# A graph attention kernel: each group's row of destinations spread by a DMA from HBM instead of by broadcast matmuls into PSUM

## The chip, the cores and the metric

One core of a Trainium2 chip runs the whole program in one launch. The metric is the device time of that launch in microseconds; the kernel before takes 2448.84 us, the median of 3 runs (2448.01 to 2454.68). The changed kernel is timed in the same way on the same inputs.

## What is computed

A two-layer graph transformer over 3125 nodes (D = 128, 8 heads of 16) and 100000 edges, sorted by destination, plus one self loop per node; a last residual and layer norm follow. Cut to what matters:

```python
for l in range(L):                       # L = 2
    xn = _layernorm(x, ln1_g[l], ln1_b[l])
    deg = segment_sum(1, src); deg = (deg - deg.mean()) / (std(deg) + 1e-06)
    xp = xn + xn @ Wpos[l] + bpos[l] + deg[:, None] * Wdeg[l][0] + bdeg[l]
    q, k, v = (xp @ Wq[l] + bq[l]), (xp @ Wk[l] + bk[l]), (xp @ Wv[l] + bv[l])
    att = clip(einsum('ehd,ehd->eh', q[dst], k[src]) / 4, -50, 50)
    alpha = softmax of att over the edges of one dst
    aggr = segment_sum(v[src] * alpha, dst)
    x = x + (aggr @ Wo[l] + bo[l])
    h = gelu(_layernorm(x, ln2_g[l], ln2_b[l]) @ W1[l] + b1[l])
    x = x + (h @ W2[l] + b2[l])
return _layernorm(x_first + x)
```

## The kernel before, in words

The nodes stand in NT = 25 tiles of 128 rows, `x` and `qkv` in SBUF throughout. The edges are cut into NG = 98 groups of GE = 1024 (8 chunks of 128). Each engine has its own instruction stream, written out by hand, and the streams meet through counting semaphores only.

Before the layers, the two edge rows are loaded (SP, L352 and L353), node degrees are counted by one-hot matmuls (L956), and for each group the first and last destination tile are found; a (group, tile) pair is numbered, and `pair_words` reads from a table how many pairs each group has (244 pairs in the 196 groups of both layers, 1.24 tiles a group). A layer then runs:

1. Dense start: normalise, transpose and project each tile to q, k, v (L1010, L1016). SP stores k and v to a table in HBM, five tiles at a time (L382, ten stores over both layers). ScalarE and VectorE split q into three bf16 parts (`q_parts`).
2. The edge stage, over the 98 groups:
   - GpSimd (L452) issues, for each group, eight indirect DMAs that gather 128 rows of 1 KB (k and v of the sources) into one of SLOTS = 4 buffers of `kv`. It waits for `idx_ready` and, for a buffer's reuse, for `msg_done` of the group four earlier.
   - TensorE `broadcast_rows` (L1035): the group's 1024 destination numbers stand in one partition of `dst_hi` and `dst_lo` (multiples of 128 and the rest, both exact in bf16). A `pick` matrix that is one in that row spreads them over 128 partitions, four matmuls of 512 columns into two PSUM banks. It is issued two groups ahead, after `picked` and after `dist_done` says that the banks are free. Groups 0 to 97 have it; the last two steps of the loop issue none.
   - ScalarE `one_hots` (L563, L566): for each pair, |destination - node| (`dist`), then relu(1 - that), which gives the one-hot `hotT`; before it `pick_rows` (L535) prepares `pick` for two groups ahead.
   - TensorE `gather_q` (L1048): 24 bf16 matmuls a pair give q[dst] in PSUM.
   - VectorE: product with gathered k (L830), sum over a head (L835), clip (L842 to L845); the second one-hot `hot` (L812); after ScalarE's exp (`weights`, L570) the product with v (L854), which raises `msg_done`.
   - TensorE `sum_pair` (L1062): 8 fp32 matmuls a pair (16 records) add the group's messages to its destination tile; VectorE adds the result to `acc` (L808).
3. Dense end: quotient, output projection (L1101, L1106), second layer norm, the two matrices of the feed-forward part (L1114, L1120), with GpSimd adding biases (L466).

ScalarE's order in the edge stage is: exp of group g, one-hots of group g + 2, exp of group g + 1, and so on. SP has nothing to do in the edge stage, but for the second copy of x (L386, L387), which overwrites the q part of `qkv` in layer 1 once that isn't read any more and is waited for (`first_in`) by VectorE before the feed-forward part of layer 1.

Of the kernel before, what the change touches and what calls it, by code (L numbers as in the profile page):

```python
# [21 lines left out]
BF16 = mybir.dt.bfloat16  # L22
# [16 lines left out]
SLOTS = 4  # L39
UN = 5  # L40
# [22 lines left out]
def gnn_program(nc, x_d, src_d, dst_d, W, out_d):  # L63
    ctx = ExitStack()
    with ctx:
# [24 lines left out]
        dst_hi = sb("dst_hi", [NG, GE], BF16)  # L90
        dst_lo = sb("dst_lo", [NG, GE], BF16)
# [13 lines left out]
        pick = sb("pick", [NG, 2, P], BF16)  # L105
# [51 lines left out]
        tmp_i = row_buf(5, I32)  # L157
        tmp_j = row_buf(6, I32)
# [34 lines left out]
        dst_rows = ps[:, 6:8, :].rearrange("p b n -> p (b n)")  # L193
# [22 lines left out]
        dst_split = sem("dst_split")  # L216
        dst_parts = sem("dst_parts")
# [41 lines left out]
        row_ready = sems("row_ready")  # L259
# [16 lines left out]
        picked = sems("picked")  # L276
# [72 lines left out]
        def _(sp):  # L349
# [22 lines left out]
            for l in range(L):  # L372
# [3 lines left out]
                load(b2_bc[:, l, :], W["b2"][l, :].partition_broadcast(P), kept_in)  # L376
            for l in range(L):

                table = kv_tab[l][:, :].rearrange("(t p) d -> p t d", p=P)
                with sp.Fori(0, NU) as i:  # L380
                    sp.wait_ge(qkv_done[l], UN * i + UN)
                    sp.dma_start(table[:, bass.ds(UN * i, UN), :], qkv[:, bass.ds(UN * i, UN), D:3 * D]).then_inc(tab_out[l], 16)  # L382
            sp.wait_ge(self_msg, L * NU)
# [19 lines left out]
        def _(pool):  # L403
            pool.memset(src_i, -1).then_inc(rows_clear, 1)
            pool.memset(dst_i, -1).then_inc(rows_clear, 1)
            pool.memset(x[:, NT - 1, :], 0.0).then_inc(x_clear, 1)
# [63 lines left out]
        def _(act):  # L470
# [21 lines left out]
            act.wait_ge(dst_split, 1)  # L492
            nc.scalar.activation(dst_hi[:, :], tmp_i, ACT.Copy, scale=float(P)).then_inc(dst_parts, 1)
            nc.scalar.activation(dst_lo[:, :], tmp_j, ACT.Copy).then_inc(dst_parts, 1)
# [24 lines left out]
            for l in range(L):  # L519
# [13 lines left out]
                def pick_rows(g):  # L533

                    nc.scalar.activation(pick[:, bass.ds(g % 2, 1), :], spread(ident[0:NG, at(g)], 2, P), ACT.Copy).then_inc(picked[l], 1)  # L535

                pick_rows(0)
                pick_rows(1)

# [14 lines left out]
                def one_hots(word, d, g):  # L554
# [3 lines left out]
                    act.wait_ge(row_ready[l], g + 1)  # L558
                    pick_rows(g + 2)
                    with act.Fori(a, b) as pr:  # L560
                        t = tile_of(act, pr, shift)
                        act.wait_ge(hotT_ready[l], pr + 1)
                        nc.scalar.activation(dist[:, :], dst_rows, ACT.Abs, bias=neg_node[:, at(t)]).then_inc(dist_done[l], 1)  # L563
# [10 lines left out]
                one_hots(word, 0, 0)  # L574
# [574 lines left out]
```

## Time and profile before

| | us |
|---|---|
| median of 3 runs (all: 2454.68, 2448.84, 2448.01) | 2448.84 |
| span of the profiled execution | 2449.8 |
| TensorE matmul busy | 1621.6 (66%) |
| TensorE weight load busy | 1408.2 (57%) |
| VectorE busy | 1418.8 (58%) |
| ScalarE busy | 807.7 (33%) |
| GpSimd busy | 1603.8 (65%) |
| data moved by DMA | 219.86 MB, 90 GB/s |

The page gives the span of one profiled execution, which is 1.0 us above the median of the runs; the page gives no time for what lies around the span. A busy share is an average over stages: the dense stages and the edge stage have different limits. So the page is read from its part 4, the chain that ended last, and then by asking what each engine's idle time ended with. PE is TensorE, PEld its weight loads, DVE is VectorE, ACT ScalarE, POOL GpSimd, SP SyncE; a trailing q marks an engine's sequencer. A busy GpSimd does not move the gathered data; it prepares the descriptors, and the DMA engines move the rows.

### The profile page before, as it was taken

Reading aid. Unit: us, or ns where it says so; the run is one execution under the profiler, and the core shown is the slowest. Engines: PE = TensorE matmul, PEld = TensorE weight load, DVE = VectorE, ACT = ScalarE, POOL = GpSimd, SP = SyncE. Lnnn points to the kernel's source line nnn. Section 1 sums busy time; section 2 is a strip of 40 time slices with the busy share of each in tenths; the row PEclk is TensorE's granted clock in tenths of the full one; section 3 lists DMA queues with packets and bytes.
Section 4 is the critical chain, followed back from the end, with each engine's and each line's share of the span. In section 5 each row is a group of like instructions: output and inputs, shape, how many; then the busy total and the mean of one; then the engine's idle time right before and its main releaser. Section 6 shows DMA issues by size and latency. Waiting matters only on the chain.

```text
span 2449.8 us, 47166 instructions
## 1 busy us (share of the span) xinstructions
PE 1621.6 (66%) x12557; PEld 1408.2 (57%) x12558; DVE 1418.8 (58%) x2438; ACT 807.7 (33%) x1355; POOL 1603.8 (65%) x1686
## 2 busy tenths in 40 slices
PE   0995656666666666666687555666666666676767
PEld 0983555555555555666675455555555656665667
DVE  3448555555556666666655655555555555565664
ACT  0004323233333333333356322333333333333326
POOL 2005777777777777777713777777777777777721
PEclk9997878887788888888888787778888888888878
DMA  1103333333333333333301433333333333333310
GB/s 48 24 1 95 105 101 103 102 102 101 105 101 101 102 103 102 102 104 101 103 1 65 125 101 101 103 101 103 103 101 101 102 103 102 102 105 101 103 37 27
DMA packets 92154, 219.86 MB, mean 90 GB/s; under 512 B 27615, under 2 KB 40068, under 8 KB 92106
## 3 DMA queue, kind: packets, MB, share of 16 engines
q0 software_dynamic: 75072, 205.10, 29.0%
q1 hardware_dynamic: 17034, 14.14, 1.9%
q8 instruction: 28, 0.46, 0.1%
q14 instruction: 20, 0.16, 0.0%
HBM read 210.98 MB, written 8.15 MB: 89 GB/s over the span
## 4 chain that ended last, share of the span: by engine, by line
POOL 61%; issue 21%; PE 11%; DVE 2%; DMA 2%; SPq 1%; POOLq 1%; DVEq 0%; ACT 0%; ACTq 0%
POOL kv L452 61%; PE ps L956 4%; PE ps L1114 2%; PE ps L1120 2%; PE ps L1016 1%; DMA x<-in_x 1%; SPq L353 1%; PE ps L1062 1%; DMA kv<-kv_tab,idx 0%; PE ps L1010 0%; DVE stats L626 0%; PE ps L1106 0%; DVE qkv L750 0%; DMA kv_tab<-qkv 0%; DVE x L897 0%
## 5 line engine op out<-in xcount | busy, mean ns | idle before, releaser
L452 POOL DMA_INDIRECT kv<-kv_tab,idx x1564 | 1539.0, 984 | 494.2 <-issue 475.2
L1062 PE MATMUL ps<-msg,hot 128*128 128x136 f32 x3904 | 754.7, 370 | 669.1 <-DVE msg L854 557.5
L1062 PEld LDWEIGHTS ps<-msg,hot 128*128 128x128 f32 x3904 | 700.9, 268 | 768.4 <-issue 768.0
L830 DVE TENSOR_TENSOR prod<-kv,ps 128x1024 f32<-128x1024 f32 x196 | 239.4, 1221 | 705.3 <-DMA kv<-kv_tab,idx 696.6
L1048 PE MATMUL ps<-q_parts,hotT 128*128 x5856 | 423.4, 235 | 58.8 <-issue 42.0
L1048 PEld LDWEIGHTS ps<-q_parts,hotT 128*128 x5856 | 402.8, 108 | 81.4 <-issue 68.1
L570 ACT ACTIVATE msg<-att 128x64 f32<-128x64 f32 x196 | 50.2, 256 | 1112.8 <-DVE att L845 1108.8
L812 DVE TENSOR_TENSOR hot<-node_row,dst_col 128x1024 f32 (+1 forms) x244 | 299.2, 1226 | 97.0 <-issue 97.0
L563 ACT ACTIVATE dist<-ps,neg_node 128x1024 bf16<-128x1024 f32 x244 | 271.9, 1114 | 51.9 <-issue 37.2
L566 ACT ACTIVATE hotT<-dist 128x1024 bf16 x244 | 257.8, 1057 | 44.1 <-ACT dist L563 44.1
L835 DVE TENSOR_REDUCE dots<-prod 128x64 f32<-128x1024 f32 x196 | 239.1, 1220 | 0.3
L854 DVE TENSOR_TENSOR msg<-kv,msg 128x1024 f32<-128x1024 f32 x196 | 238.9, 1219 | 0.1
L1035 PE MATMUL ps<-dst_hi,pick 98*128 98x512 bf16 x392 | 150.5, 384 | 6.0 <-issue 5.0
L1035 PE MATMUL ps<-dst_lo,pick 98*128 98x512 bf16 x392 | 149.8, 382 | 0.0
L466 POOL TENSOR_TENSOR x<-x,b_bc 128x128 f32 x50 | 22.7, 456 | 139.5 <-ACT z L487 139.5
L535 ACT ACTIVATE pick<-ident 98x128 bf16 (+1 forms) x200 | 61.4, 308 | 158.2 <-issue 96.6
L956 PE MATMUL ps<-q_parts 128*64 128x49 bf16 x784 | 98.2, 302 | 4.7 <-DVE q_parts L704 4.7
L956 PEld LDWEIGHTS ps<-q_parts 128*64 128x64 bf16 x784 | 97.2, 221 | 7.0 <-DVE q_parts L704 4.8
L443 POOL TENSOR_TENSOR x<-x,bo_bc 128x128 f32 x50 | 24.9, 500 | 92.3 <-ACT z L487 91.9
L808 DVE TENSOR_TENSOR acc<-acc,ps x244 | 70.3, 288 | 14.9 <-PE ps L1062 8.3
L703 DVE TENSOR_TENSOR q_parts<-q_parts,qkv 128x1792 bf16<-128x1792 bf16 x28 | 30.6, 1092 | 64.5 <-PE ps L956 63.9
L601 ACT ACTIVATE kv<-ps,b1f 128x128 f32<-128x128 f32 x200 | 57.2, 369 | 20.5 <-PE ps L1114 20.5
(156 smaller groups left out, 1058.8 us busy)
## 6 DMA issues: line engine op xcount, KB each, us to landing
kv<-kv_tab,idx POOLq DMA_INDIRECT x1564
kv_tab<-qkv SPq DMA_DIRECT2D x10, 640.0 KB, 3.3
out<-x SPq DMA_DIRECT2D x4, 320.0 KB
hot<-in_L_gnn_W SPq DMA_DIRECT2D x2, 256.0 KB
w<-in_L_gnn_W SPq DMA_DIRECT2D x2, 256.0 KB, 3.3
kv<-in_src SPq DMA_DIRECT2D x1, 388.0 KB
kv<-in_dst SPq DMA_DIRECT2D x1, 388.0 KB
out<-x SPq DMA_DIRECT2D x1, 256.0 KB
```

Of the source, the lines that this page charges most:

```text
L452: pool.indirect_dma_start(kv[:, u, c, :], None, kv_tab[l][:, :], bass.IndirectOffsetOnAxis(ap=idx[:, u, c:c + 1], axis=0)).then_inc(kv_in[ ...
L563: nc.scalar.activation(dist[:, :], dst_rows, ACT.Abs, bias=neg_node[:, at(t)]).then_inc(dist_done[l], 1)
L566: nc.scalar.activation(hotT[:, bass.ds(pr % 2, 1), :], dist[:, :], ACT.Relu, bias=1.0, scale=-1.0).then_inc(hotT_ready[l], 1)
L808: nc.vector.tensor_tensor(acc[:, at(t), :], acc[:, at(t), :], agg[:, bass.ds((end + 1) % 2, 1), :], ALU.add).then_inc(evac_done[l], 1)
L812: nc.vector.tensor_tensor(hot[:, u % 2, :, :], spread(node_row[:, bass.ds(t * P, P)], 1, GC), dst_col[:, :, at(g)].broadcast_to([P, GC, P] ...
L830: nc.vector.tensor_tensor(prod[:, :].rearrange("p (c d) -> p c d", d=D), kv[:, u, :, 0:D], qd[u % 2].rearrange("p (c d) -> p c d", d=D), A ...
L835: nc.vector.tensor_reduce(dots[:, :], prod[:, :].rearrange("p (n d) -> p n d", d=HD), AX.X, ALU.add).then_inc(dot_done[l], 1)
L854: nc.vector.tensor_tensor(half[:, :, 0:D].rearrange("p c (h d) -> p c h d", d=HD), kv[:, u, :, D:2 * D].rearrange("p c (h d) -> p c h d", ...
L956: last = MM(cnt, hot_lo[b][:, :, c], hot_hi[b][:, :, c], start=False, stop=True, skip_group_check=True)
L1035: last = MM(dst_rows[:, cut], pick[:, gp, :], part[:, cut], start=start, stop=not start)
L1048: last = MM(qd[u % 2][:, c * P:(c + 1) * P], hotT[:, bass.ds(pr % 2, 1), c * P:(c + 1) * P], q_parts[:, at(t), k * D:(k + 1) * D], start=f ...
L1062: last = MM(agg[:, bass.ds(pr % 2, 1), :], hot[:, u % 2, c, :], msg[:, u % 2, c, :], start=(c == 0), stop=(c == GC - 1))
```

## The change

The destination row no longer goes through TensorE. The 1024 int32 numbers of group g are read from HBM by one DMA on SP whose source has a step of zero over 128 partitions, so each partition receives the same 4 KB (512 KB a group, 196 loads over both layers). They land in one of ROWS = 3 buffers of a new SBUF tile `dst_rows`, [128, 3, 1024] int32. ScalarE's `dist` reads that buffer, as int32 from SBUF instead of fp32 from PSUM. `pick`, `dst_hi`, `dst_lo`, the two VectorE instructions that split the numbers (L656, L657), the two of ScalarE that convert them (L493, L494) and all `broadcast_rows` are gone. GpSimd clears `dst_rows` at the start. SP issues the load of group g after the exp of group g - 4 (the first three of a layer at once, behind that layer's table stores), and its later work, the next layer's stores and the second copy of x, stands behind the loads. ScalarE's loop is unrolled by six groups instead of four.

```diff
+ROWS = 3
+TURN = 2 * ROWS
-        dst_hi = sb("dst_hi", [NG, GE], BF16)
-        dst_lo = sb("dst_lo", [NG, GE], BF16)
+        dst_rows = sb("dst_rows", [P, ROWS, GE], I32)
-        pick = sb("pick", [NG, 2, P], BF16)
-        dst_rows = ps[:, 6:8, :].rearrange("p b n -> p (b n)")
+        rows_in = [sems(f"rows_in{l}_", ROWS) for l in range(L)]
...
+            sp.wait_ge(rows_clear, 3)
             for l in range(L):
 
                 table = kv_tab[l][:, :].rearrange("(t p) d -> p t d", p=P)
                 with sp.Fori(0, NU) as i:
                     sp.wait_ge(qkv_done[l], UN * i + UN)
                     sp.dma_start(table[:, bass.ds(UN * i, UN), :], qkv[:, bass.ds(UN * i, UN), D:3 * D]).then_inc(tab_out[l], 16)
+                for g in range(NG):
+                    r = g % ROWS
+                    if g >= ROWS:
+                        sp.wait_ge(exp_done[l], max(1, g - ROWS))
+                    elif l:
+                        sp.wait_ge(exp_done[l - 1], NG)
+                    n = min(GE, E - g * GE)
+                    sp.dma_start(dst_rows[:, r, 0:n], dst_d[g * GE:g * GE + n].partition_broadcast(P)).then_inc(rows_in[l][r], 16)
...
+            pool.memset(dst_rows[:, :, :], -1).then_inc(rows_clear, 1)
...
-            act.wait_ge(dst_split, 1)
-            nc.scalar.activation(dst_hi[:, :], tmp_i, ACT.Copy, scale=float(P)).then_inc(dst_parts, 1)
-            nc.scalar.activation(dst_lo[:, :], tmp_j, ACT.Copy).then_inc(dst_parts, 1)
...
-                def pick_rows(g):
-
-                    nc.scalar.activation(pick[:, bass.ds(g % 2, 1), :], spread(ident[0:NG, at(g)], 2, P), ACT.Copy).then_inc(picked[l], 1)
-
-                pick_rows(0)
-                pick_rows(1)
...
-                def one_hots(word, d, g):
+                def one_hots(word, d, r, n):
 
                     a = word(d - 1)[0]
                     b, shift = word(d)
-                    act.wait_ge(row_ready[l], g + 1)
-                    pick_rows(g + 2)
+                    act.wait_ge(rows_in[l][r], 16 * (n + 1))
                     with act.Fori(a, b) as pr:
                         t = tile_of(act, pr, shift)
                         act.wait_ge(hotT_ready[l], pr + 1)
-                        nc.scalar.activation(dist[:, :], dst_rows, ACT.Abs, bias=neg_node[:, at(t)]).then_inc(dist_done[l], 1)
+                        nc.scalar.activation(dist[:, :], dst_rows[:, r, :], ACT.Abs, bias=neg_node[:, at(t)]).then_inc(dist_done[l], 1)
...
-            nc.vector.tensor_single_scalar(tmp_i, dst_i, 7, ALU.arith_shift_right)
-            nc.vector.tensor_single_scalar(tmp_j, dst_i, P - 1, ALU.bitwise_and).then_inc(dst_split, 1)
...
-                def broadcast_rows(gp, g, a):
-
-                    pe.wait_ge(picked[l], g + 1)
-                    if a is not None:
-                        pe.wait_ge(dist_done[l], a)
-                    for half in range(2):
-                        cut = slice(512 * half, 512 * half + 512)
-                        for part, start in ((dst_hi, True), (dst_lo, False)):
-                            last = MM(dst_rows[:, cut], pick[:, gp, :], part[:, cut], start=start, stop=not start)
-                    last.then_inc(row_ready[l], 1)
```

## Rows read from the trace of the kernel before

**Rows 1.** The page, part 4: shares of the chain that ended last, by engine.

```profile
POOL 61%; issue 21%; PE 11%; DVE 2%; DMA 2%; SPq 1%; POOLq 1%; DVEq 0%; ACT 0%; ACTq 0%
```

**Rows 2.** Groups by line: L452: busy us, mean ns | idle before, releasers.

```profile
L452 POOL DMA_INDIRECT kv<-kv_tab,idx x1564 | 1539.0, 984 | 494.2 <-issue 475.2 <-DMA kv_tab<-qkv 18.3 <-DVE idx L728 0.6
```

**Rows 3.** Line L452: count, duration min/median/max in ns.

```profile
L452 POOL DMA_INDIRECT kv<-kv_tab,idx x1564: 942/946/2000, 217.2 to 2347.0; - x196
```

**Rows 4.** The chain in order of time, layer 0: start us, us, what.

```profile
360.05 1.97 POOL kv L452
...
401.43 1.96 POOL kv L452
```

**Rows 5.** The page, part 5: groups of L563, L1035 and L535.

```profile
L563 ACT ACTIVATE dist<-ps,neg_node 128x1024 bf16<-128x1024 f32 x244 | 271.9, 1114 | 51.9 <-issue 37.2
...
L1035 PE MATMUL ps<-dst_hi,pick 98*128 98x512 bf16 x392 | 150.5, 384 | 6.0 <-issue 5.0
...
L535 ACT ACTIVATE pick<-ident 98x128 bf16 (+1 forms) x200 | 61.4, 308 | 158.2 <-issue 96.6
```

**Rows 6.** Groups by line, small ones: L493, an int32 row read from SBUF.

```profile
L493 ACT ACTIVATE dst_hi<-kv 98x1024 bf16<-98x1024 int32 x1 | 1.1, 1057 | 38.7 <-DVE kv L657 38.7
```

**Rows 7.** Timeline, start of the kernel: start us, us, engine, line, what, idle.

```profile
0.81 0.95 POOL L404 MEMSET kv<- 98x1024 int32 x1 [0.29 <-POOLq L1135]
...
38.76 4.01 POOL L430 TENSOR_SCALAR kv<-kv 98x1024 f32<-98x1024 f32 x1 [27.87 <-DVE kv L655]
...
42.99 4.93 DVE L626 BATCH_NORM_STATS2 stats<-x 128x6 f32<-128x128 f32 x25 [2.28 <-DMA x<-in_x]
```

**Rows 8.** The page, DMA issues by line: KB each, median us to landing.

```profile
kv_tab<-qkv SPq DMA_DIRECT2D x10, 640.0 KB, 3.3
...
bo_bc<-in_L_gnn_bo SPq DMA_DIRECT2D x2, 64.0 KB, 3.6
```

**Rows 9.** Layer 0's start: ScalarE's first `dist`, VectorE's first product, 33rd gather.

```profile
226.45 1.11 ACT L563 ACTIVATE dist<-ps,neg_node 128x1024 bf16<-128x1024 f32 x1 [0.19 <-issue]
...
235.91 1.22 DVE L830 TENSOR_TENSOR prod<-kv,ps 128x1024 f32<-128x1024 f32 x1 [1.19 <-issue]
...
258.75 0.95 POOL L452 DMA_INDIRECT kv<-kv_tab,idx  x1 [0.30 <-issue]
```

**Rows 10.** Layer 1's end: exp of group 93, VectorE's first zT copy.

```profile
2314.97 0.26 ACT L570 ACTIVATE msg<-att 128x64 f32<-128x64 f32 x1 [3.99 <-DVE att L845]
...
2385.78 0.61 DVE L909 COPY zT<-ps 128x128 f32<-128x128 f32 x2 [1.16 <-PE ps L1010]
```

**Rows 11.** DMA queues from 1360 to 1362 us, and GpSimd's gathers in it.

```profile
q1 hardware_dynamic: 295, 0.60, 104.6%
...
1359.21 0.95 POOL L452 DMA_INDIRECT kv<-kv_tab,idx  x1 [0.30 <-issue]
1360.46 0.97 POOL L452 DMA_INDIRECT kv<-kv_tab,idx  x1 [0.30 <-issue]
```

**Rows 12.** The page, part 3: the gathers' queue: packets, MB, share of 16 engines.

```profile
q0 software_dynamic: 75072, 205.10, 29.0%
```

**Rows 13.** Timeline of TensorE at the ends of layer 0 and layer 1.

```profile
1230.23 5.64 PE L1062 MATMUL ps<-msg,hot 128*128 128x136 f32 x32 [2.68 <-DVE acc L808]
...
2348.83 3.99 PE L1062 MATMUL ps<-msg,hot 128*128 128x136 f32 x16 [5.17 <-DVE msg L854]
...
2355.46 6.77 PE L1062 MATMUL ps<-msg,hot 128*128 128x136 f32 x32 [2.63 <-DVE acc L808]
```

**Rows 14.** Stretch: busy of PE, PEld, DVE, ACT, POOL; clock, DMA share, GB/s.

```profile
2350.00:2355.00 5.00, 2.82 (x13) 2.50 (x12) 4.08 (x7) 0.26 (x1) 0.00 (x0) 0.50 0.00 0
```

**Rows 15.** DMA from 121 to 122 us: packets and queues, share of 16 engines.

```profile
DMA packets 106, 0.05 MB, mean 48 GB/s; under 512 B 12, under 2 KB 106, under 8 KB 106
...
q1 hardware_dynamic: 106, 0.05, 50.8%
```

**Rows 16.** Stretch, L452 alone: POOL busy us (x count); clock, DMA share, GB/s.

```profile
217.00:235.80 18.80, 14.70 (x13) 0.50 0.29 84
```

## Prediction: the destination rows by DMA

> **What bounds the kernel now.** I read the chain of work that ended last first: GpSimd's gathers (L452) are 61% of it and "issue" another 21% [rows 1]. The reader is to see one engine there, with all of TensorE at 11%. Next the waits of that engine. Before its 1564 gathers it idled 475.2 us on "issue", its own time between two instructions, 18.3 us on the stored table at the two layer starts, and 0.6 us on anything the edge loop computes [rows 2]. It never waits for `msg_done`, the only semaphore by which the edge work could hold it. The same row gives 984 ns a gather; with 475.2 / 1560 = 305 ns between them a group of eight takes 8 x 1.289 = 10.3 us, and the two layers 1539.0 + 475.2 = 2014 of the 2449.8 us. The middle gather takes 946 ns [rows 3]; one in 32 takes about 1.96 us, 41.4 us after the last such one [rows 4]: 49 x 1.0 = 49 us in all, a fixed toll. So the edge stage is a train of gathers with three followers; the rest of the kernel, 435 us, is dense work that this change leaves alone but for the edges below.
>
> **What goes.** Four matmuls a group: two lines of 150.5 us, of which one stands here, so 300 us of TensorE in 196 groups, 1.5 us a group [rows 5]. ScalarE loses the 200 `pick` copies, 61.4 us [rows 5]. None of it is on the chain, since a follower that ends earlier waits longer for the same gather. Worth 0. `dist` now reads int32 from SBUF instead of fp32 from PSUM: the old one takes 1114 ns [rows 5], and an int32 row of 1024 out of SBUF took ScalarE 1057 ns [rows 6], so 0 to -0.06 us on an engine that is busy a third of the time: 0. At the start VectorE loses L656 and L657 (about 2 us), after which it stood 2.28 us for x anyway; GpSimd gains a memset of 128 x 3072 int32, three times the 952 ns of L404 = 2.9 us, ahead of work after which it idled 27.9 us [rows 7]. Both are covered; without cover they would be -2 and +2.9 us.
>
> **What comes: 196 loads of 512 KB on SP.** The trace has no such load. The nearest by size is the table store, 640 KB in 3.3 us; the nearest by pattern is the bias spread of 64 KB, 3.6 us [rows 8]. I take 3.3 us to land, because size is the larger difference. The upper bound comes with the rival below: 10.9 us. Need and supply: row g is issued after the exp of group g-4 and read by ScalarE after the exp of group g-2, two groups or 20.6 us later. Even the upper bound lands in time, so the new wait `rows_in` costs 0. Queued behind that wait on ScalarE are the exp of the next group and so `msg_done`; one_hots(g) sits before the exp of group g-1, hence a row would have to be later than about 28 us before anybody noticed, and GpSimd only after its four slots ran out.
>
> On the SP queue the loads pass three things. (1) The first three rows of a layer stand behind the last table store, so they can't delay its start, but they share its last moments: 0 to 1 us on the first gather of each layer, I take 0.5, +1 us for two. They land near 217 us; ScalarE first needs one at 226.45, VectorE's first product is at 235.91, and GpSimd would need that product's group only for its 33rd gather at 258.75 [rows 9]. Cover of 9 us, then of 20 more. (2) The second layer's table stores stand behind row 97 of the first, which goes out at the exp of group 93, four groups before the stage ends; between that and the first store lies the whole dense part. 0. (3) The second copy of x (L386, L387) used to go out early in layer 1 and now waits for the exp of group 93, at 2314.97. At the table store's rate its 1.6 MB take 8 us, and VectorE first asks for it at its copy at 2385.78 [rows 10]: 60 us of cover, 0.
>
> **What the loads do to the gathers.** This is the term that is not covered: all 1564 gathers are on the chain, and 5 ns on each is 7.8 us, 0.3% of the time and about what a measurement of this kernel can tell from no change. The trace holds one test. From 1360 to 1362 us the copy of x keeps all 16 DMA engines full (104.6%), and the two gathers issued beside it took 0.95 and 0.97 us [rows 11]: 0 to 24 ns above the 946 of a quiet one; I take the middle, 12. The gathers' own 205.10 MB cost 29.0% of the engines [rows 12], that is 0.29 x 2449.8 / 196 = 3.6 us a group; at the same cost per byte a row takes 3.6 / 2 = 1.8 us, 17% of a group. So 12 ns x 0.17 x 1564 = +3 us, with bounds 0 and 24 x 0.17 x 1564 = 6 us.
>
> Here the Trainium skill speaks against the change: "DMA: Bandwidth & Descriptors", section "Issuing engines are not separate DMA queues", says that DMAs of SP and of GpSimd run on the same 16 engines and interleave. Taken as a cost in full, 1.8 us a group would be added wherever the gathers' movement were the bound; here preparing them is. The same skill's "SBUF — State Buffer", section "Who interferes with whom", would make this term exactly zero, as it lets no DMA disturb a computing engine. By the first 196 x 1.8 = 353 us more, by the second none; the 0.95 us gather beside a full set of engines sides with the second.
>
> **The tails.** After the last gather of a layer nothing new runs. The TensorE clock is in play: the last 32 matmuls of L1062 took 5.64 us in layer 0 and 6.77 in layer 1, while 16 in a stretch granted 0.50, the lower level (1.2 GHz), took 3.99 [rows 13, 14], so all 32 there would be 7.98: +2.3 and +1.2 us if the engine, now idle more, is granted the low level throughout, 0 if not. The last two groups had no broadcast before either, and this tail ran mostly at the low level already, so I take 0; bounds 0 to +3.5.
>
> **Sum.** Against the profiled span of 2449.8: 0 (removed) + 1 (first gathers) + 3 (gathers beside rows) + 0 (tails) = 2453.8. The median of the runs lies 1.0 below the span, so 2452.8, said as 2453. With every bound against it, 2 + 6 + 3.5, it is 2460; with every one for it 2449.
>
> **The rivals.**
> *Held engines, slower.* All 128 descriptors of a row read the same 4 KB, 16 engines at once. If that address is the limit, packets of the gathers stand behind stalled ones. The slowest broadcast traffic in the trace is from 121 to 122 us, when only bias spreads are left: 48 GB/s [rows 15]. At that rate a row takes 0.524 MB / 48 GB/s = 10.9 us, and with the gathers' 3.6 the engines need 14.5 us a group: +4.2 x 196 = +820 us, 3273. It decides from 10.3 - 3.6 = 6.7 us a row, 78 GB/s. Against it: in that very window the engines were busy only 50.8%, which scales to 94 GB/s and 5.5 us, below the point. A half measure of it: were the gathers' movement the bound, each row would add its own 1.8 us, 353 in all, 2803. Chance of both 0.07.
> *Slower preparation of gathers.* If a gather beside a row grows not by 12 ns but as the first 13 of layer 0 do (14.70 / 13 = 1131 ns, 185 above the quiet one [rows 16]), the price is 0.185 x 0.17 x 1564 = +49 us in place of the +3, 2499. For: rows come at a fixed point of each group, so the same gather would always be hit. Against: the copy of x did nothing of the kind, and those 13 had no SP transfer beside them but VectorE's bulk work. Chance 0.10.
> *Fewer disturbed gathers, faster.* Mean 984 less the toll of 49 / 1564 = 31 ns leaves 953, 7 above the quiet 946: 10 us in all are small disturbances. If these came from the traffic that goes, -10 us, 2443. They fall on whatever VectorE does at that moment, and that stays. Chance 0.04.
>
> **How the numbers follow.** Forecast 0.77 (2447 to 2460 as its own range: the bounds of the sum and 2 us of scatter below), held engines 0.07, slower preparation 0.10, faster 0.04, something unseen 0.02. The forecast's upper end passes 2456 in a few cases, 0.02. Faster by over 0.3%: 0.05. Slower: 0.07 + 0.10 + 0.02 + 0.01 = 0.20. Same: 0.75. For eight in ten the range takes all of the forecast and the lower part of the slower preparation: 2443, where the faster case lies, to 2475.
>
> **What would show it.** Right: GpSimd's waits still "issue" alone, 1564 gathers near 984 ns, the 41 us rhythm unchanged; TensorE 300 us less busy, VectorE's wait on the gathers as long as before; `rows_in` in no row of ScalarE's waits; TensorE's L1035 and ScalarE's L535 gone; the DMA engines' share of the edge stage up by about 0.17. The rival of held engines would show as packets that take several times longer, ScalarE waiting for `dst_rows` and GpSimd for VectorE's `msg`; slower preparation as a mean of L452 above 1.0 us with no wait on it. The prediction falls if one gather is lengthened by the load beside it, for nothing else stands on the chain.

## The result: 2451.8 us after, 2448.7 us before

| | before | after |
|---|---|---|
| median of 20 runs, us | 2448.73 | 2451.76 |
| lowest and highest, us | 2446.64, 2454.68 | 2450.40, 2454.37 |
| profiled execution: its time, its span, us | about 2451.6 (span 2449.8) | 2451.1 (span 2449.3) |
| granted TensorE clock, profiled execution | 0.834 | 0.794 |

The ratio is 1.0013, with a 95% interval from 1.0007 to 1.0019: 3.0 us slower, or 0.13%, inside the band of 0.3% that the prediction called "same". The prediction was 2453, range 2443 to 2475. The time of an execution lies 1.7 to 1.8 us above its span in every run, and that of the profiled one of before is worked out so. The last five runs below (e8 to e12) ran on two other chips, on which every kernel, the one before too, took about a third longer, so each is compared only with the kernel before on its own chip.

The chain that ended last, after:

```profile
POOL 61%; issue 21%; PE 11%; DVE 2%; DMA 1%; SPq 1%; POOLq 1%; DVEq 0%; ACT 0%; ACTq 0%
```

Read beside [rows 1]: the same picture. Next the groups by line of GpSimd, VectorE and ScalarE (busy us, mean ns | idle before, and what ended it):

```profile
L456 POOL DMA_INDIRECT kv<-kv_tab,idx x1564 | 1538.7, 984 | 495.0 <-issue 475.5 <-DMA kv_tab<-qkv 19.2 <-DVE idx L723 0.3
...
L825 DVE TENSOR_TENSOR prod<-kv,ps 128x1024 f32<-128x1024 f32 x196 | 239.3, 1221 | 706.0 <-DMA kv<-kv_tab,idx 703.8 <-PE ps L1030 1.2 <-DVE acc L790 0.9
...
L556 ACT ACTIVATE dist<-dst_rows,neg_node 128x1024 bf16<-128x1024 int32 x244 | 280.1, 1148 | 209.1 <-issue 195.4 <-ACT hotT L559 13.8
```

GpSimd's row is that of [rows 2] to within 0.3 us of busy time and 0.9 of waiting, which is on the table at the two layer starts. VectorE waits 703.8 us for gathers (696.6 before), so it is as early as it was. ScalarE's `dist` has no wait on `dst_rows`: the idle time that `pick` and the broadcast used to take is now "issue". And each `dist` takes 1148 ns where it took 1114 [rows 5]: with an int32 row in SBUF as its input it is 3% slower than with an fp32 one in PSUM, not a little faster.

The traffic, from the page's parts 3 and 6 (packets, MB, share of 16 engines; KB each, us to landing):

```profile
q0 software_dynamic: 75072, 205.10, 27.6%
q1 hardware_dynamic: 45258, 116.55, 15.1%
...
dst_rows<-in_dst SPq DMA_DIRECT2D x194, 512.0 KB, 4.1
```

A row lands 4.1 us after its issue. SP's queue carried 14.14 MB at 1.9% of the engines before; the 102 MB that came are worth 13.2%, that is 0.132 x 2449.3 / 196 = 1.65 us of all 16 engines a row. From 300 to 1200 us the engines (the two last columns: DMA share, GB/s; before them the clock) stood at 0.35 and 102 GB/s before, and after:

```profile
300.00:1200.00 900.00, 527.00 (x4422) 502.56 (x4421) 537.03 (x857) 265.36 (x309) 686.26 (x702) 0.78 0.50 153
```

The broadcast is gone from TensorE, and the busy time of the engine fell from 1621.6 to 1481.4 us, by 140 and not by 300. The two rows of 150 us [rows 5] hold matmuls that overlap: each is on record for 0.38 us, and the next starts 0.22 us after it. Together they kept TensorE busy for 204.6 us, 1.04 us a group, as the kernel before shows over its whole span (PE's busy time is the second figure behind the stretch):

```profile
704.93 0.38 PE L1035 MATMUL ps<-dst_hi,pick 98*128 98x512 bf16 x1
705.15 0.38 PE L1035 MATMUL ps<-dst_lo,pick 98*128 98x512 bf16 x1
...
0.00:2450.00 2450.00, 204.64 (x784) 68.15 (x784) 0.83 0.31 90
```

And some of that was given back, for the row for `sum_pair` grew from 370 ns a matmul to 384:

```profile
L1044 PE MATMUL ps<-msg,hot 128*128 128x136 f32 x3904 | 793.9, 384 | 823.2 <-DVE msg L849 682.3
```

An engine with 205 us less to do was granted a lower clock (0.83 to 0.78 in this stretch), and that line took 39 us more (754.7 to 793.9). The gathers didn't notice. The last one starts at 2348.7 us (2347.0 before [rows 3]), which is 1.7 us later, while this execution is 0.5 us the shorter one: a pair of single executions doesn't place the 3 us.

### The profile page after: what moved, and what is told of

The parts are those of the page before. It is cut to its first block, busy times and chain, and to the rows that moved or that the text cites. A ratio compares the mean times of both kernels' runs of the same rounds, so it can differ in the third digit from the quotient of the medians.

```text
span 2449.3 us, 45172 instructions
## 1 busy us (share of the span) xinstructions
PE 1481.4 (60%) x11773; PEld 1389.2 (57%) x11774; DVE 1414.9 (58%) x2436; ACT 751.3 (31%) x1152; POOL 1606.0 (66%) x1687
## 3 DMA queue, kind: packets, MB, share of 16 engines
q0 software_dynamic: 75072, 205.10, 27.6%
q1 hardware_dynamic: 45258, 116.55, 15.1%
## 4 chain that ended last, share of the span: by engine, by line
POOL 61%; issue 21%; PE 11%; DVE 2%; DMA 1%; SPq 1%; POOLq 1%; DVEq 0%; ACT 0%; ACTq 0%
POOL kv L456 61%; PE ps L951 4%; PE ps L1091 2%; PE ps L1097 2%; PE ps L1011 1%; DMA x<-in_x 1%; SPq L347 1%; PE ps L1044 1%; PE ps L1005 1%; DVE stats L623 0%; DMA kv_tab<-qkv 0%; PE ps L1083 0%; DVE x L892 0%; DMA kv<-kv_tab,idx 0%; DVE qkv L745 0%
## 5 line engine op out<-in xcount | busy, mean ns | idle before, releaser
L456 POOL DMA_INDIRECT kv<-kv_tab,idx x1564 | 1538.7, 984 | 495.0 <-issue 475.5
L1044 PE MATMUL ps<-msg,hot 128*128 128x136 f32 x3904 | 793.9, 384 | 823.2 <-DVE msg L849 682.3
L1044 PEld LDWEIGHTS ps<-msg,hot 128*128 128x128 f32 x3904 | 740.7, 282 | 859.7 <-issue 859.6
L825 DVE TENSOR_TENSOR prod<-kv,ps 128x1024 f32<-128x1024 f32 x196 | 239.3, 1221 | 706.0 <-DMA kv<-kv_tab,idx 703.8
L1030 PE MATMUL ps<-q_parts,hotT 128*128 x5856 | 423.4, 236 | 50.8 <-issue 49.1
L563 ACT ACTIVATE msg<-att 128x64 f32<-128x64 f32 x196 | 50.2, 256 | 1167.3 <-DVE att L840 1150.6
L556 ACT ACTIVATE dist<-dst_rows,neg_node 128x1024 bf16<-128x1024 int32 x244 | 280.1, 1148 | 209.1 <-issue 195.4
L830 DVE TENSOR_REDUCE dots<-prod 128x64 f32<-128x1024 f32 x196 | 239.1, 1220 | 0.3
L1091 PE MATMUL ps<-zT,w1g 128*128 128x128 f32 x400 | 57.0, 289 | 0.0
L838 DVE TENSOR_SCALAR clipped<-dots 128x64 f32<-128x64 f32 x196 | 56.0, 286 | 0.0
L1091 PEld LDWEIGHTS ps<-zT,w1g 128*128 128x128 f32 x400 | 52.5, 205 | 0.5 <-DVE zT L904 0.5
```

The lines of the kernel that those rows point to most:

```text
L456: pool.indirect_dma_start(kv[:, u, c, :], None, kv_tab[l][:, :], bass.IndirectOffsetOnAxis(ap=idx[:, u, c:c + 1], axis=0)).then_inc(kv_in[ ...
L556: nc.scalar.activation(dist[:, :], dst_rows[:, r, :], ACT.Abs, bias=neg_node[:, at(t)]).then_inc(dist_done[l], 1)
L825: nc.vector.tensor_tensor(prod[:, :].rearrange("p (c d) -> p c d", d=D), kv[:, u, :, 0:D], qd[u % 2].rearrange("p (c d) -> p c d", d=D), A ...
L830: nc.vector.tensor_reduce(dots[:, :], prod[:, :].rearrange("p (n d) -> p n d", d=HD), AX.X, ALU.add).then_inc(dot_done[l], 1)
L1030: last = MM(qd[u % 2][:, c * P:(c + 1) * P], hotT[:, bass.ds(pr % 2, 1), c * P:(c + 1) * P], q_parts[:, at(t), k * D:(k + 1) * D], start=f ...
L1044: last = MM(agg[:, bass.ds(pr % 2, 1), :], hot[:, u % 2, c, :], msg[:, u % 2, c, :], start=(c == 0), stop=(c == GC - 1))
```

## The experiments

The theory: preparing the gathers on GpSimd sets the time; the 196 loads and the removed matmuls both lie beside it. What has to be tested is (a) that nothing of the removal is worth anything here, and why, (b) that the loads are as harmless as they look and from where they stop being so, (c) where the 3.0 us come from.

### e1: the loads alone, added to the kernel before

```diff
+ROWS = 2
+        rows_sb = sb("rows_sb", [P, ROWS, GE], I32)
+                for g in range(NG):
...
+                    sp.dma_start(rows_sb[:, r, 0:n], dst_d[g * GE:g * GE + n].partition_broadcast(P)).then_inc(rows_in[r], 16)
```

> The kernel before with the 196 loads of 512 KB added on SP, into a tile of two buffers that nobody reads (each load also waits until the last one into its buffer has landed, since two buffers instead of three stand free). All broadcast matmuls and pick copies stay; the second copy of x waits behind the loads as in the changed kernel. Theory A (the 3 us that the change costs come from the loads: they share the last moments of the table store and the gathers' descriptors): 2451 to 2453, ratio to before about 1.0013, gathers still 984 ns. Theory B (the 3 us come from TensorE, which is idler and is granted the lower clock more often, where the dense stages and the layers' tails stand on it): 2448 to 2449.5, ratio 1.000. A mean gather above 990 ns would speak for the slower preparation of gathers after all.

Measured: 2450.21 us, ratio 1.0008, interval 0.9999 to 1.0018, so +1.2 us with zero at its edge. That lies between the two theories (2451 to 2453, and 2448 to 2449.5) and decides for neither. The gathers stay at 984 ns with the engines at 0.50 in place of 0.35, and the table's wait is 19.1 us in place of 18.3:

```profile
L467 POOL DMA_INDIRECT kv<-kv_tab,idx x1564 | 1538.7, 984 | 494.9 <-issue 475.5 <-DMA kv_tab<-qkv 19.1 <-DVE idx L743 0.3
```

The term "12 ns x 0.17 x 1564 = +3 us" of the prediction isn't seen: 1538.7 us of gathers with 102 MB of rows beside them, 1539.0 without. The other profiles with the rows (e2, e3, e6) read 1539.6, 1541.3 and 1536.6, so single profiles tell this to about 2 us.

### e2: the matmuls alone, put back into the kernel after

```diff
+                def broadcast_rows():
+                    for half in range(2):
+                        cut = slice(512 * half, 512 * half + 512)
+                        for part, start in ((dst_hi, True), (dst_lo, False)):
+                            MM(bcast[:, cut], part[:, 0:P], part[:, cut], start=start, stop=not start)
...
+                    if ahead:
+                        broadcast_rows()
```

> The changed kernel with four broadcast matmuls a group put back on TensorE, of the same shapes and at the same place in its order, into the two freed PSUM banks; nobody waits for them or reads them, and pick stays out (a slice of the bf16 rows serves as weights). Theory A (loads): 2451 to 2453, as the changed kernel, granted clock back at about 0.83. Theory B (TensorE's clock): back to 2448 to 2449.5, with the granted clock at about 0.83 and the stretches after the last gather of each layer as short as before.

Measured: 2451.85 us, ratio 1.0013 (1.0004 to 1.0022), granted clock 0.83. The clock of before is back, and the 3 us are still there. So the lower clock isn't their cause; and 784 matmuls put back cost nothing, the other side of their removal being worth nothing.

### e3: the kernel after once more

> The changed kernel itself, on the same chip as the two beside it, so that a difference of 3 us can be read from runs that share everything. Both theories: 2450.4 to 2454.4, ratio 1.0007 to 1.0019. If it comes out within 1 us of before here, there is no 3 us to explain and the difference was one between chips.

Measured: 2453.16 us, ratio 1.0015 (1.0006 to 1.0024), as expected. The difference is small but it comes back.

### e4 and e5: half the gathers, in the kernel before and in the kernel after

This takes GpSimd's cover away: with four gathers in place of eight a group, who is next? Both kernels leave out half of the gathered rows, so what they compute is not the layer's result; every instruction behind the gathers stays.

```diff
+HALF = 4
-                    for c in range(chunks):
+                    for c in range(GC if first else HALF):
-                        dve.wait_ge(kv_in[l][u], 16 * (GC * i + (LAST_CHUNKS if last_group else GC)))
+                        dve.wait_ge(kv_in[l][u], 16 * (HALF * i + GC))
```

> The kernel before with the cover taken away: GpSimd gathers four of the eight chunks of a group (all eight only for the first four groups of a layer), so its train would take 5.2 us a group; the upper four chunks of kv keep the rows of earlier groups. Everything else is computed. If the reading is right that only the gathers bind, the followers now do: VectorE needs 1.22 x 3 + 1.23 x 1.24 and the small ones, some 7 us a group, TensorE 7.5 us of matmuls at the higher clock with the broadcasts. I expect 8 to 9 us a group, some 2100 to 2250 us in all. If the time stays near 2449, something else than the gathers held the edge stage.

> The changed kernel with the same half gathers. Now the removed TensorE work (1.5 us a group) is not covered by the gathers. If TensorE is the next bound, up to 1.5 x 196 = 300 us less than the half-gather kernel before; if the chain of VectorE is, about the same as that one (within 30 us). I expect something between: 50 to 200 us less.

Measured: e4 1822.31 us (ratio 0.7442), e5 1764.61 us (0.7210). e4 came out some 300 us below the 2100 to 2250 that were expected: layer 0's train of gathers takes 7.0 us a group there and not 8 to 9. The difference of 57.7 us is within what was expected of e5; it is 3.2%, and here the change is worth having. The chains, first e4's, then e5's:

```profile
PE 49%; ACT 18%; issue 13%; DVE 7%; DVEq 4%; POOL 3%; ACTq 2%; DMA 2%; SPq 1%; POOLq 0%
```

```profile
PE 31%; DVE 28%; issue 18%; DVEq 15%; POOL 4%; DMA 2%; SPq 1%; ACT 1%; ACTq 0%; POOLq 0%
```

And ScalarE's `pick` in e4, which stands in the queue for TensorE's broadcast:

```profile
L536 ACT ACTIVATE pick<-ident 98x128 bf16 (+1 forms) x200 | 61.4, 308 | 575.6 <-PE ps L1036 573.1 <-issue 2.5
```

With GpSimd at 3% of the chain, the kernel before is bound by a loop through TensorE and ScalarE, in which the broadcast (L1036) is 8% of the chain. Take it out and VectorE has the largest part of the chain (28%, and 15% for its queue), with TensorE's `sum_pair` (13%) next. From 400 to 800 us its busy time, the third of the five, is 358.85 us out of 400, and it was 345.48 in e4:

```profile
400.00:800.00 400.00, 299.58 (x3024) 279.99 (x3024) 358.85 (x580) 183.08 (x213) 237.34 (x238) 0.91 0.50 156
```

So the change frees 206 us of TensorE and 61 of ScalarE, and even with half the gathers gone only 58 us of them come out. VectorE is next, one step behind. And TensorE gives some of it back here too: its granted clock goes from 0.965 to 0.910, and a matmul of `sum_pair` from 285 to 314 ns, 91 us on that line. In the kernel as it is both engines are behind GpSimd.

### e6: each row asked for only after the exp of two groups before

```diff
-                        sp.wait_ge(exp_done[l], max(1, g - ROWS))
+                        sp.wait_ge(exp_done[l], max(1, g - 1))
```

> The changed kernel with each load issued two groups later: behind the exp of group g - 2 instead of g - 4, so right before ScalarE wants it. ScalarE must then wait about 4.1 us a group for the row (its landing time), 800 us of waits in all. My reading of the cover (a row may be late until the exp of the next group, 10 us later) says that this costs nothing: 2451 to 2455. The rival, that a wait of ScalarE delays the exp and through it the gathers, says 1 to 4 us a group, 2650 to 3200.

Measured: 2451.95 us, ratio 1.0015 (1.0005 to 1.0025), the same as the kernel after. Now ScalarE does wait:

```profile
L556 ACT ACTIVATE dist<-dst_rows,neg_node 128x1024 bf16<-128x1024 int32 x244 | 280.1, 1148 | 906.6 <-DMA dst_rows<-in_dst 886.9 <-ACT hotT L559 13.8 <-issue 5.9
```

887 us of waiting on the row, 4.5 us a group, and none of it on the chain, in which ScalarE stands at 0% as before. Both were expected (800 us, and 2451 to 2455). This is the plainest lesson of the case in how a wait is read: the largest entry of an engine's waits may be worth nothing.

### e7: three more loads of 512 KB for each group

```diff
+        spare = nc.dram_tensor("spare", [P, 3, GE], I32)
...
+                    for e in range(3):
+                        after(sp, spare_in[e], 16 * (l * NG + g))
+                        sp.dma_start(spare[:, e, 0:n], dst_d[g * GE:g * GE + n].partition_broadcast(P)).then_inc(spare_in[e], 16)
```

> The changed kernel with three more loads of the same destination row a group, each of 512 KB into a scratch in HBM, issued by SP behind the row's own load and each waiting only for its predecessor of the group before. It prices the DMA engines: gathers 3.6 us and rows 1.6 us a group are the shares of the changed kernel; four rows make 3.6 + 6.4 = 10.0 us beside a train of 10.3, right at the point where I put the rival of the held engines. If gathers are bound by their preparation alone until the engines are full, 2451 to 2500; if the gathers' preparation grows with the traffic beside it (185 ns a gather, say), 2700 or more, with a mean gather well above 984 ns; if the movement becomes the bound, VectorE's wait shows and the gathers' mean stays at 984.

Measured: 2505.05 us, ratio 1.0233 (1.0216 to 1.0250), +56 us against the kernel before and +53 against the one after.

```profile
300.00:1200.00 900.00, 494.95 (x4291) 470.38 (x4289) 518.62 (x838) 260.16 (x302) 691.61 (x685) 0.77 0.98 300
```

```profile
L463 POOL DMA_INDIRECT kv<-kv_tab,idx x1564 | 1586.2, 1014 | 495.0 <-issue 471.5 <-DMA kv_tab<-qkv 19.2 <-DVE idx L730 4.3
```

The three more loads go into a scratch in HBM, where the row's own load goes into SBUF. The expected ranges were 2451 to 2500 for gathers bound by their preparation alone, and 2700 or more for a preparation that grows with the traffic; it came out 5 us above the first. The DMA engines are full (0.98, 300 GB/s), and GpSimd's idle time before the gathers is the same 495.0 us: what grew is the gather itself, 1538.7 to 1586.2 us, or 47.5 us. This profiled execution took 2498.0 us, 46.9 more than the profiled one of after, so the gathers are all of it. It isn't every gather. The middle one takes 946 ns as before, but 146 of the 1564 take more than 1.15 us, against 55 in the kernel before and 55 in the one after.

What makes a gather long stands beside it on VectorE. Two of e7, and one of e4, whose DMA engines stood at 0.26:

```profile
710.81 1.23 DVE L814 TENSOR_TENSOR hot<-node_row,dst_col 128x1024 f32 x1 [0.26 <-issue]
711.12 1.73 POOL L463 DMA_INDIRECT kv<-kv_tab,idx  x1 [0.30 <-issue]
...
724.02 1.23 DVE L814 TENSOR_TENSOR hot<-node_row,dst_col 128x1024 f32 x1 [0.30 <-issue]
724.49 1.58 POOL L463 DMA_INDIRECT kv<-kv_tab,idx  x1 [0.30 <-issue]
```

```profile
407.48 1.22 DVE L813 TENSOR_TENSOR hot<-node_row,dst_col 128x1024 f32 x1 [0.29 <-issue]
407.72 1.79 POOL L453 DMA_INDIRECT kv<-kv_tab,idx  x1 [0.30 <-issue]
```

Each of the three began while `hot` was running, and each ended 0.81 or 0.82 us after `hot` did (712.85 and 712.04, 726.07 and 725.25, 409.51 and 408.70). Counted over the whole traces, 145 of the 146 long gathers of e7 are of this kind, 54 of 55 in the kernel before, 54 of 55 after, 103 of 104 in e4 and 98 of 99 in e5: when they began, VectorE was running a `tensor_tensor` with both inputs in SBUF (`hot` or `msg`, or one of the dense start), and they ended 0.81 to 0.84 us behind it. The one left over in each is the first gather of the kernel. VectorE's other instructions do nothing of the kind: in the kernel before 369 gathers began with more than 0.33 us of one left, mostly the product (whose second input is in PSUM) or the sum over a head, and none of them is long, there or in the other four traces.

So the full DMA engines lengthen no gather by themselves. They move VectorE against GpSimd. In the kernels before and after, the product (L830, L825) starts 1.9 to 2.0 us after the last gather of its group in the middle half of the groups, and `hot` then mostly starts 0.2 to 0.3 us into a gather, where it does no harm. In e7 the rows land late, the product starts 5.1 to 6.0 us after, and 123 long gathers began inside a `hot` (31 in the kernel before, 26 after). What the long gathers of this kind take beyond 946 ns each is 54 us more than in the kernel after, and all the others take 7 us less: together the 47.5. In e4 and e5 it is GpSimd that waits for VectorE, which shifts the two in the same way: a mean gather takes 1034 and 1041 ns, with the engines at 0.26 and 0.50 (from 400 to 800 us). The rival "slower preparation of gathers" thus names a real lengthening, but it comes from VectorE's instructions, and the traffic has a part in it only by shifting them. This is read from the traces; no run moved the two engines against each other and left all else alone.

### e8 to e10: which part costs the 3 us, and double the traffic

e8 keeps three row loads a layer, so that later groups read the row of another group; e9 adds one load a group (into a buffer of SBUF); e10 puts the first three rows of a layer ahead of its table store:

```diff
 e8
-                for g in range(NG):
+                for g in range(ROWS):
...
-                    act.wait_ge(rows_in[l][r], 16 * (n + 1))
+                    act.wait_ge(rows_in[l][r], 16)
 e10
+                for r in range(ROWS):
+                    if l:
+                        sp.wait_ge(exp_done[l - 1], NG)
+                    sp.dma_start(dst_rows[:, r, :], dst_d[r * GE:r * GE + GE].partition_broadcast(P)).then_inc(rows_in[l][r], 16)
                 with sp.Fori(0, NU) as i:
...
-                for g in range(NG):
+                for g in range(ROWS, NG):
```

> The kernel after with only the first three rows of each layer loaded (6 loads instead of 196); every later group reads whichever row lies in its buffer, so its destinations are not its own, and everything else runs as in the kernel after. This looks for the 3.0 us (1.0013) that the change costs. Theory A, the traffic of the loads: without 190 of the 196 loads the time falls back to the kernel before, 2448.8 to 2449.5 us, ratio 1.000, and the share of the DMA engines from 300 to 1200 us falls from 0.50 to about 0.35. Theory B, it lies in what replaces the matmuls (ScalarE's reading of integer rows, 1148 instead of 1114 ns, and the edits of the start) or in the table's wait: the ratio stays at 1.001 or above, 2451 to 2452.5 us.

> The kernel after with one more 512 KB load of the same row per group, into a buffer that nobody reads: double the traffic of the change. Theory A, each 100 MB of loads lengthens the preparation of gathers a little, in proportion: three more per group gave 53 us, so one more gives 15 to 20 us, 2467 to 2472 us, ratio 1.0075 to 1.010, gathers at about 993 ns. Theory C, the engines take this amount without effect and the 53 us came only as their share neared full (0.98): 2452 to 2455 us, ratio 1.0015 to 1.0025, gathers at 984 to 985 ns, share of DMA about 0.65.

> The kernel after with the first three rows of each layer loaded ahead of that layer's table store instead of behind it (layer 1's after the last exponential of layer 0, well over 50 us before the table is stored). If the wait for the table before the first gathers (19.2 us in both layers together, 18.3 in the kernel before) is longer because three 512 KB rows share its last moments, it goes back to 18.3 us and the time falls by about 1 us, to 2450.8 us, ratio 1.0008 to 1.001. Rival, the rows have nothing to do with it: 19.2 us and 2451.8 us, ratio 1.0013, remain.

Measured: e8 3309.08, e9 3310.39, e10 3306.26 us, and on the same chip the kernel before 3347.16 us (3322.79 to 3365.85), where the two chips of e1 to e7 had it at 2449. The ratios are 0.9898 (0.9861 to 0.9934), 0.9902 (0.9865 to 0.9938) and 0.9875 (0.9840 to 0.9910). None of the expected times can be held against these, for the bound is another one. TensorE and GpSimd in e10:

```profile
L1031 PE MATMUL ps<-q_parts,hotT 128*128 x5856 | 629.4, 255 | 947.0 <-issue 944.1 <-ACT hotT L560 2.0
```

```profile
L457 POOL DMA_INDIRECT kv<-kv_tab,idx x1564 | 1528.4, 977 | 1328.1 <-DVE msg L850 834.3 <-issue 473.3 <-DMA kv_tab<-qkv 19.0
```

In the kernel after, the matmuls of `gather_q` idle 49.1 us on "issue"; here 944.1 us. The timeline shows single matmuls with 0.4 to 1.8 us of nothing between them:

```profile
470.77 0.27 PE L1031 MATMUL ps<-q_parts,hotT 128*128 x1 [1.20 <-issue]
472.21 0.27 PE L1031 MATMUL ps<-q_parts,hotT 128*128 x1 [1.18 <-issue]
```

TensorE stood idle with nothing in the profile to wait for, and GpSimd, whose gathers are as quick as ever (977 ns), stood 834 us for VectorE's `msg`. In all five traces of these chips 30 to 39% of the chain is "another core or an unknown queue", which is in no chain of the other chips: VectorE's product alone waits 1093.7 us for it in e10. Why it was so no profile tells. One reading does survive, since it lies in the dense start, ahead of all this: the wait of layer 0's first gather on the table. e10 first, then e8:

```profile
  DMA kv_tab<-qkv: 11.6, 1
```

```profile
  DMA kv_tab<-qkv: 12.1, 1
```

It is 12.1 us in the kernel after and in e8, e9, e11 and e12, all with three rows behind the table store, and 11.6 in e10, which has them ahead, as in the kernel before (11.6). The pair of e4 and e5 says the same, 11.6 without rows and 12.2 with them. So the prediction's 0.5 us for rows that share the last moments of the store holds in layer 0. In layer 1 the same wait reads 6.8 before, 7.1 after and 7.4 in e10, but 7.1 also in e4, which has no rows: no cost of the rows is seen there.

### e11 and e12: e8 and e9 once more

> The kernel of e8 again (only the first three rows of each layer are loaded, later groups read whichever row lies in their buffer), since in its job every kernel, the one before too, took 3306 to 3347 us with TensorE issuing one matmul in some 0.7 us, so that GpSimd's gathers didn't set the time. On a chip where the kernel before takes about 2449 us: theory A, the traffic of the loads costs the 3.0 us: ratio 0.9998 to 1.0003, 2448.5 to 2449.5 us. Theory B, what replaces the matmuls costs them (integer rows read by ScalarE, the start, the table's wait): ratio 1.001 or above, 2451 to 2452.5 us.

> The kernel of e9 again (one more 512 KB load of the same row per group, into a buffer that nobody reads), for the same reason. Theory A, the gathers' preparation lengthens in proportion to the traffic: 2467 to 2472 us, ratio 1.0075 to 1.010, gathers at about 993 ns. Theory C, the 53 us of three more loads came only as the share of the DMA engines neared full: 2452 to 2455 us, ratio 1.0015 to 1.0025, gathers at 984 to 985 ns, share of DMA about 0.65 from 300 to 1200 us.

Measured: e11 3250.45 us, e12 3280.06, the kernel before 3284.34 (3252.68 to 3322.63); ratios 0.9918 (0.9886 to 0.9949) and 0.9990 (0.9957 to 1.0023). It was yet another chip with the same picture as that of e8 to e10, here the matmuls of `gather_q` in e11, and the question that the two runs were made for stays unanswered.

```profile
L1030 PE MATMUL ps<-q_parts,hotT 128*128 x5856 | 641.0, 257 | 868.0 <-issue 863.3 <-ACT hotT L559 2.4 <-DVE prod L825 0.5
```

Of these five kernels without the broadcast four are 0.8 to 1.3% faster than the kernel before on their chip, and one is the same. That fits a bound in which each instruction of TensorE has a price and 784 matmuls fewer are a gain, as e5 against e4 is for another such bound. It is argued, not shown: on neither chip is there a trace of the kernel before or a run of the unedited kernel after, and the same kernel gave 0.9902 as e9 and 0.9990 as e12.

## Why the prediction was right, step by step

*What bounds the kernel now.* Right: the chain is the same to a percent, and the half-gather pair shows the rest of it, since 748 gathers less (816 are left) take 627 us off and only then do the followers bind. The toll of the long gathers was misread: 32 of them take about 1.96 us in the kernel before, not 49, it isn't fixed, and it comes from VectorE. The one at 360.05 us [rows 4] began 0.07 us after `msg` did and ended 0.83 us after `msg` ended (361.19 us):

```profile
359.98 1.21 DVE L854 TENSOR_TENSOR msg<-kv,msg 128x1024 f32<-128x1024 f32 x1
```


*What goes, worth 0.* Right, and e2 shows it from the other side. The amount was wrong, at no price here: 300 us, and "TensorE 300 us less busy" as a sign of being right, add up durations that overlap. The matmuls kept the engine busy for 205 us, and its busy time fell by 140. Also wrong: the step put `dist` at 0 to -0.06 us, from a 98-partition copy of another shape [rows 6], and it came out at +0.034 (1148 against 1114 ns). On an engine that idles it is worth nothing, but the sign came from a row whose shape and function differed.

*What comes.* The landing was taken as 3.3 us, from the table store as the row nearest in size; it is 4.1, and the 64 KB bias spread, nearest in pattern, had said 3.6 [rows 8]. The pattern counted for more than I gave it, though neither row reaches 4.1. The cover of 20.6 us made that idle, and e6 shows how idle: asking for each row two groups later turned the cover into 887 us of ScalarE's waiting at no price. The first rows beside the table store: taken +0.5 us a layer, measured +0.9 us for both (18.3 to 19.2 us). In layer 0 the +0.5 is theirs (e10, and e5 against e4); in layer 1 e4 has as much without any row. The second copy of x went out at 2316.41 us, 1.4 us after the time that the step took for it, and nothing waited for it.

*What the loads do to the gathers.* The size was off: +3 us forecast, none measured (1538.7 against 1539.0 us in the profiles, 1538.7 in e1). I had made it from two gathers beside the copy of x, 0.95 and 0.97 us, and took the middle of a rounding: the two rows said little more than "not 1.0". The engine time of a row, forecast 1.8 us, is 1.65. The share of DMA rose by 0.15 (0.17 forecast). By the Trainium skill ("DMA: Bandwidth & Descriptors", section "Issuing engines are not separate DMA queues") the two kinds of traffic share the 16 engines; the shares in the page agree, 27.6 and 15.1%, and it had no price while preparation was the bound. The rule of the Trainium skill's "SBUF — State Buffer", section "Who interferes with whom", by which no DMA disturbs a computing engine, agrees at 0.50 of the engines. At 0.98 the busy time of GpSimd's gathers grows by 47.5 us (e7), which doesn't speak against that rule: the gathers that grew are those that began beside an instruction of VectorE.

*The tails.* Forecast 0 with 0 to +3.5: the last 32 matmuls took 6.62 us in layer 0 and 6.33 in layer 1, against 5.64 and 6.77 [rows 13], so +1.0 and -0.4 in one pair of profiles:

```profile
1230.23 6.62 PE L1044 MATMUL ps<-msg,hot 128*128 128x136 f32 x32 [2.62 <-DVE acc L803]
...
2357.20 6.33 PE L1044 MATMUL ps<-msg,hot 128*128 128x136 f32 x32 [2.75 <-DVE acc L803]
```

*The sum.* It put +4 us on the median of the runs; +3.0 was measured. That is nearer than its parts were, and by luck: of the +1 for the first gathers 0.5 us is shown, the 3 us of the gathers aren't there, and some 2.5 us lie where no step of mine looked. The offset of 1.0 us between span and median was itself a sum that I didn't take apart: an execution takes 1.8 us more than its span, and the profiled one was 2.9 us above the median of 20. It did no harm only because it leads back to the median.

*What stays open.* Of the 3.0 us 0.5 are layer 0's first gather. The rest isn't found. It isn't the TensorE clock (e2), no profile shows longer gathers beyond their scatter of 2 us, and it isn't the row's landing (e6). The loads by themselves give +1.2 us (e1), an interval that holds both 0 and most of the rest; the dense part between the layers, from the start of layer 0's last gather to that of layer 1's first, reads 117.4 us before and 119.4 after, but 117.4 in e1, 118.1 in e2 and 116.7 in e3, so that a single profile doesn't tell 2 us. The two runs that were to split it further (e8, e11) fell on the chips with the other bound.

*The rivals.* Held engines: refuted, 1.65 us of engine time a row against the 6.7 from which it decides, even with four loads of the row at a time (one into SBUF and three into HBM in e7: 0.98 of the engines and no new idle time on GpSimd). Slower preparation: not in the change. That its +49 us is near e7's 47.5 is chance: it was priced for one row a group, and the long gathers of e7 come from VectorE's place in time. Its argument against itself, that the slow ones had VectorE's bulk work beside them, was the right lead. Fewer disturbed gathers: refuted, there are 55 of more than 1.15 us in both kernels, and the reason given for that was right: they fall on what VectorE does at that moment, and that stayed.

## What to carry to other kernels

Before an engine is relieved, look whether it is on the chain, and if it isn't, who would be next once it were: here 266 us of freed work (205 of TensorE, 61 of ScalarE) were worth nothing beside the gathers, and 58 us when half the gathers were gone. Two rows of one engine may overlap, so take what a removal frees from the busy time of their line and not from the sum of the rows. Replacing compute by DMA is harmless while the engines have room; when they are full it can cost without a single new wait, by instructions of the issuing engine that get longer. Read the largest durations as well as the mean, and look at what the other engines run at the moment at which a long one begins. An effect near 0.1% is beyond what single profiles can place: executions of one kernel differ by more.

## What the runs showed of the hardware that was not expected

- A 4 KB row of HBM spread over 128 partitions (512 KB) lands in 4.1 us and costs 1.65 us of all 16 DMA engines. Four such loads a group (three of them into HBM), with the gathers, filled the engines at 300 GB/s, and GpSimd's idle time stayed at 495.0 us.
- A gather that GpSimd begins while VectorE runs a `tensor_tensor` of 128x1024 fp32 with both inputs in SBUF ends 0.81 to 0.84 us after that instruction does, and so takes up to 2.0 us in place of 946 ns (54 of the 55 gathers of more than 1.15 us before, 145 of 146 in e7). Where VectorE begins second, by 0.2 to 0.3 us, the gather mostly isn't lengthened.
- How many gathers are hit depends on how the two engines lie in time and not on the traffic: 55 of 1564 with the DMA engines at 0.35 and at 0.50, 104 of 816 at 0.26 (e4), 146 of 1564 at 0.98 (e7).
- ScalarE's `dist` takes 1148 ns from an int32 row of 1024 in SBUF and 1114 from an fp32 one in PSUM.
- TensorE without the broadcasts is granted 0.78 instead of 0.83 from 300 to 1200 us, and one unchanged line of its matmuls takes 39 us more; with the broadcasts back (e2) it is 0.81, and 34 of the 39 us are gone.
- The same kernel took 2449 us on two chips and 3284 and 3347 on two others. In the traces from there, all of edited kernels, TensorE's matmuls are 0.4 to 1.8 us apart on "issue", while VectorE's product, ScalarE's `dist` and the gathers take what they did (1217, 1148 and 977 ns in e10). What bounds a kernel can differ from one chip to the next, and so may the sign of a change.
